# High and low fp32r parts for the experts' gate and up products, and 71 tiles instead of 72

## The reference

```python
def reference(x, cond, Wq, Wo, router_w, gate_up_w, down_w, shared_gate_w, shared_up_w, shared_down_w):
    return x + ffn(attention(x, cond, Wq, Wo))      # x: 16 x 256 x 512, float32

def attention(x, mask, Wq, Wo):                     # 8 heads of 32, over the 512 positions
    q = x.transpose(0, 2, 1) @ Wq.T                 # queries, keys and values are the same q
    logits = (scale * q_h @ q_h.T * mask_k + (1 - mask_k) * -1e30) * mask_q
    return ((softmax(logits) @ q_h) @ Wo.T).transpose(0, 2, 1)

def ffn(h):                                         # 4096 tokens of 512, 8 experts of 256, 2 a token
    shared = silu(x @ shared_gate_w) * (x @ shared_up_w) @ shared_down_w
    top_val, top_idx = top_k(x @ router_w, 2)
    probs = zeros.at[top_idx].set(sigmoid(top_val))
    gu = einsum('etd,edf->etf', probs.T[:, :, None] * x[None], gate_up_w)
    gate, up = split(gu, 2)
    return shared + einsum('eti,eid->etd', silu(gate) * up, down_w).sum(0)
```

## Time and profile before

| | us |
|---|---|
| median of the runs | 1277.66 |
| the profiled execution | 1280.32 |
| its span | 1278.2 |
| PE busy | 1192.3 (93%) |
| POOL busy | 782.2 (61%) |
| DVE busy | 696.6 (55%) |
| ACT busy | 491.7 (38%) |

### The profile page before, as it was taken

The page is one execution under the profiler, slowest core; times in us unless marked ns, Lnnn a source line. Parts: engine busy times, 40 slices in busy tenths (PEclk is TensorE's granted clock), DMA queues, the critical chain, the costliest instruction groups (busy, mean ns, idle before and its releaser), DMA issues. The chain is left out here.

```text
span 1278.2 us, 20836 instructions
## 1 busy us (share of the span) xinstructions
PE 1192.3 (93%) x5372; PEld 648.1 (51%) x5373; DVE 696.6 (55%) x1243; ACT 491.7 (38%) x922; POOL 782.2 (61%) x526
## 2 busy tenths in 40 slices
PE   4999999999999999999977999699999999999995
PEld 2444545455444555455437999544444444444442
DVE  4776676776766766667615744234444443343333
ACT  1465665665565656556543222011111111111110
POOL 1487877877877877778860277435545445444443
PEclk8799999999999999999988999899999999999998
DMA  6467667677676676685515995534454555556551
GB/s 185 137 169 210 187 171 205 175 183 205 175 195 184 171 200 190 169 215 151 151 69 199 365 359 180 170 102 139 144 162 157 174 177 173 186 184 198 190 201 50
DMA packets 116747, 230.26 MB, mean 180 GB/s; under 512 B 19230, under 2 KB 22046, under 8 KB 116704
## 3 DMA queue, kind: packets, MB, share of 16 engines
q1 hardware_dynamic: 85216, 160.35, 42.6%
q0 software_dynamic: 23936, 54.72, 14.1%
q10 hardware_dynamic: 7552, 14.68, 3.6%
HBM read 150.14 MB, written 98.39 MB: 194 GB/s over the span
## 5 line engine op out<-in xcount | busy, mean ns | idle before, releaser
L762 DVE TENSOR_REDUCE row_max<-bank 128x1 f32<-128x512 f32 x512 | 343.4, 684 | 177.4 <-PE bank L582 176.6
L695 ACT ACTIVATE probsT<-bank 128x512 f32<-128x512 f32 x512 | 300.1, 596 | 227.6 <-PE bank L594 225.5
L451 POOL TENSOR_TENSOR key_sum<-key_sum,probsT 128x1024 f32<-128x1024 f32 x128 | 299.5, 2367 | 0.4 <-ACT probsT L695 0.4
L582 PE MATMUL bank<-k_stack,q_stack 96*128 96x512 f32 x512 | 282.3, 555 | 12.8 <-DMA q_stack<-q_hi 8.1
L1506 PE MATMUL bank<-gate_up_sb,rows_T 128*128 x576 | 273.0, 597 | 1.6 <-ACT rows_T L1453 1.6
L447 POOL TENSOR_TENSOR key_sum<-probsT 128x1024 f32<-128x1024 f32 x64 | 151.3, 2377 | 129.1 <-ACT probsT L695 129.1
L594 PE MATMUL bank<-q_stack,k_stack 99*128 99x512 f32 x512 | 207.4, 406 | 1.7 <-ACT probsT L695 1.5
L1371 POOL DMA_INDIRECT out<-rows_final,slot_info x72 | 73.4, 1020 | 187.4 <-DVE rows_final L1429 185.2
L582 PEld LDWEIGHTS bank<-k_stack,q_stack 96*128 96x128 f32 x512 | 98.5, 193 | 168.4 <-DVE row_max L762 126.4
L1460 ACT ACTIVATE gated<-bank 128x256 f32<-128x256 f32 x72 | 27.6, 383 | 360.4 <-PE bank L1506 360.4
L1506 PEld LDWEIGHTS bank<-gate_up_sb,rows_T 128*128 128x128 f32 x576 | 104.5, 192 | 106.3 <-issue 106.3
(11 more groups left out here) (139 smaller groups left out, 1365.3 us busy)
## 6 DMA issues: line engine op xcount, KB each, us to landing
expert_rows_dram<-zero_rows SPq DMA_DIRECT2D x16, 1152.0 KB, 7.2
expert_rows_dram<-rows_out SPq DMA_DIRECT2D x72, 256.0 KB, 2.3
k_stack<-hi_dram SPq DMA_DIRECT2D x60, 256.0 KB, 6.6
q_stack<-hi_dram SPq DMA_DIRECT2D x60, 256.0 KB, 7.1
x_row<-in_x SPq DMA_DIRECT2D x16, 512.0 KB, 3.8
rows_ext_dram<-hid SPq DMA_DIRECT2D x16, 512.0 KB, 5.7
hidT_dram<-hidT SPq DMA_DIRECT2D x16, 512.0 KB, 3.0
tok<-hidT_dram SPq DMA_DIRECT2D x16, 512.0 KB, 5.7
```

What stands on the lines that cost most here:

```text
L451: nc.gpsimd.tensor_tensor(total, total, probs(k), ALU.add).then_inc(added, 1)
L582: nc.tensor.matmul(logit_bank[i % 2][:, :], q_stack[par][g][0:K_LOGIT, h, q * P:(q + 1) * P], k_stack[par][g][0:K_LOGIT, h, :], start=True ...
L695: nc.scalar.activation(probsT[:, j, :], key_bank[j % 2][:, :], ACT.Exp, scale=SCALE).then_inc(probs_ready, 1)
L762: nc.vector.tensor_reduce(row_max[g][:, i:i + 1], logit_bank[i % 2][:, :], AX.X, ALU.max)\
```

## The change

NT falls from 72 to 71, in all that is derived from it. The experts' gate and up weights stay in SBUF as fp32 and are split, chunk k by chunk k, while the first tiles run: ACT rounds four pieces of 128 x 1024 into `gate_up_lo[k]` (`round_pieces`), DVE replaces them by raw minus rounded (`lower_pieces`), ACT then rounds the raw weights in place (`round_in_place`). Tile n uses fp32r parts for the chunks that are split by then (one from tile 1, two from tile 3, three from 5, all four from tile 7). A split chunk is three fp32r matmuls (high x high, high x low, low x high) in place of one fp32 matmul. The rows are turned unscaled, ACT's `copy_in` makes their high part, DVE's `lower_rows` the low part. The probability is applied in silu's scale and in `combine`; `scale_rows` is gone. `turn_in(n + 1)` moves into the middle of `gate_up(n)`. DEPTH falls from 6 to 4 and AHEAD from 3 to 2. The last tile isn't stored to `expert_rows`. The text of `clear_rows` is unchanged: with NT = 71 its n is 568, r is 8, and 71 partitions are read.

```diff
-        NT = -(-(2 * TOKENS + E * (P - 1)) // (4 * P)) * 4
+        NT = (2 * TOKENS + E * (P - 1)) // P
...
-            DEPTH = 6
-            AHEAD = 3
+            DEPTH = 4
+            AHEAD = 2
+            PIECES = 4
+            EP = E // PIECES
+            FIRST_SPLIT = [2 * k + 1 for k in range(KT)]
...
+            def split_chunks(n):
+
+                return KT if not isinstance(n, int) else sum(n >= m for m in FIRST_SPLIT)
...
             @block3.vector
             def _(dve):
-                def scale_rows(n):
-                    dve.wait_ge(gathered[n % DEPTH], 16 * (n // DEPTH + 1))
-                    if n >= 2:
-                        dve.wait_ge(in_turned, n - 1)
-                    nc.vector.tensor_scalar(rows_scaled[n % 2][:, :], rows_in[n % DEPTH][:, 0, :],
-                                            slot_info[:, n, PROB:PROB + 1].bitcast(F32), None, ALU.mult).then_inc(scaled, 1)
...
+                def lower_rows(n):
+
+                    c = split_chunks(n)
+                    dve.wait_ge(in_copied, n + 1)
+                    if n >= 2:
+                        dve.wait_ge(gu_done, n - 1)
+                    nc.vector.tensor_tensor(rows_lo[n % 2][:, 0:c, :], inT_bank[n % 2][:, 0:c * P].rearrange("p (k c) -> p k c", k=c),
+                                            rows_hi[n % 2][:, 0:c, :].bitcast(F32), ALU.subtract).then_inc(in_lowered, 1)
...
+                lower_pieces(0, range(PIECES))
                 for n in range(NT + 2):
-                    if 0 <= n - 2:
+                    if 0 <= n - 2 < NT - 1:
                         add_rest(n - 2)
                     if 0 <= n - 1 < NT:
                         copy_h(n - 1)
+                    if n == NT - 1:
+                        combine(n)
                     if 0 <= n - 2:
                         add_partner(n - 2)
-                    if n < NT:
+                    if n + 1 < NT and split_chunks(n + 1):
+                        lower_rows(n + 1)
+                    if n < NT - 1:
                         combine(n)
-                    if n + 2 < NT:
-                        scale_rows(n + 2)
+                    if n < 2 * (KT - 1):
+                        lower_pieces(n // 2 + 1, range(n % 2 * PIECES // 2, (n % 2 + 1) * PIECES // 2))
 
             @block3.scalar
...
+                act.wait_ge(experts_loaded, 2 * E * 16)
+                round_pieces(0)
                 copy_in(0, 0)
-                tiles(act, step)
+                round_pieces(1)
+                for n in range(NT):
+                    if n + 1 < NT:
+                        copy_in(n + 1, n % 2 + 1)
+                    if n + 1 in FIRST_SPLIT[0:2]:
+                        round_in_place(n // 2)
+                    silu(n, n % 2)
+                    if n + 1 in FIRST_SPLIT[2:]:
+                        round_in_place(n // 2)
+                    if n in (1, 3):
+                        round_pieces(n // 2 + 2)
...
                     for k in range(KT):
-                        if k == KT // 2 and exists(n - 1):
-                            turn_h(n - 1, i - 1)
-                        w = gate_up_sb[:, bass.ds(e * KT + k, 1), :].rearrange("p o f -> p (o f)")
-                        last = nc.tensor.matmul(gu_bank[i % 2][:, :], rows_T[i % 2][:, k, :], w,
-                                                start=(k == 0), stop=(k == KT - 1))
+                        if k == KT // 2:
+                            if exists(n - 1):
+                                turn_h(n - 1, i - 1)
+                            if exists(n + 1):
+                                turn_in(n + 1, i + 1, r)
...
+                        if isinstance(n, int) and n == FIRST_SPLIT[k]:
+                            pe.wait_ge(chunk_split, PIECES * (k + 1))
+                        w_lo = gate_up_lo[k][:, bass.ds(e, 1), :].rearrange("p o f -> p (o f)")
+                        nc.tensor.matmul(dst, hi, w, start=start, stop=False)
+                        nc.tensor.matmul(dst, hi, w_lo, start=False, stop=False)
+                        last = nc.tensor.matmul(dst, lo, w, start=False, stop=stop)
                     last.then_inc(gu_done, 1)
```

More of the change, by code:

```diff
@@ L1326, in build, with tiles, piece @@
             block3 = experts.enter_context(nc.Block())
[L1328 to L1336, removed]
+            def tiles(eng, step, unroll):
+                first_round = -(-8 // unroll)
+                last_round = (NT - 2) // unroll
+                for n in range(first_round * unroll):
+                    step(n, n % unroll, n // unroll)
+                with eng.Fori(first_round, last_round) as r:
+                    for i in range(unroll):
+                        step(unroll * r + i, i, r)
+                for n in range(last_round * unroll, NT + 3):
+                    step(n, n % unroll, n // unroll)
+            def split_chunks(n):
+                return KT if not isinstance(n, int) else sum(n >= m for m in FIRST_SPLIT)
+            def piece(k, p):
+                return slice(EP * p * KT + k, (EP * (p + 1) - 1) * KT + k + 1, KT)
             def first(n, m=2):
@@ L1452, in copy_in @@
                         act.wait_ge(gu_done, n - 1)
[L1453 to L1454 removed]
+                    turned = inT_bank[i % 2][:, :].rearrange("p (k c) -> p k c", k=KT)
+                    if c < KT:
+                        last = nc.scalar.activation(rows_raw[i % 2][:, c - i % 2:, :], turned[:, c:, :], ACT.Copy)
+                    if c > 0:
+                        last = nc.scalar.activation(rows_hi[i % 2][:, 0:c, :], turned[:, 0:c, :], ACT.Copy)
@@ new lines, in copy_in, with round_pieces, round_in_place @@
+                    last.then_inc(in_copied, 1)
+                def round_pieces(k):
+                    for p in range(PIECES):
+                        nc.scalar.activation(gate_up_lo[k][:, EP * p:EP * (p + 1), :], gate_up_sb[:, piece(k, p), :], ACT.Copy)\
+                            .then_inc(piece_rounded, 1)
+                def round_in_place(k):
+                    act.wait_ge(piece_lowered, PIECES * (k + 1))
+                    if k < KT - 1:
+                        act.wait_ge(raw_used, k + 1)
+                    else:
+                        act.wait_ge(gu_done, FIRST_SPLIT[k])
+                    for p in range(PIECES):
+                        nc.scalar.activation(gate_up_hi[:, piece(k, p), :], gate_up_sb[:, piece(k, p), :], ACT.Copy).then_inc(chunk_split, 1)
@@ L1456, in silu @@
                 def silu(n, i):
                     act.wait_ge(gu_done, n + 1)
-                    if not first(n):
-                        act.wait_ge(h_done, n - 1)
-                    nc.scalar.activation(gated[i % 2][:, :], gu_bank[i % 2][:, 0:I], ACT.Silu).then_inc(silu_done, 1)
-                def step(n, i):
-                    if exists(n):
-                        silu(n, i)
-                    if exists(n + 1):
-                        copy_in(n + 1, i + 1)
-                copy_in(0, 0)
@@ L1470, in _, with step @@
             @block3.sync
             def _(sp):
-                def step(n, i):
-                    if exists(n - 2):
+                def step(n, i, r):
+                    if exists(n - 2) and not (isinstance(n, int) and n - 2 == NT - 1):
                         sp.wait_ge(out_ready, n - 1)
@@ L1477, in step @@
                             .then_inc(stored[i % 2], 16)
-                tiles(sp, step)
+                tiles(sp, step, 2)
                 for i in range(2):
-                    sp.wait_ge(stored[i], 8 * NT)
+                    sp.wait_ge(stored[i], 16 * ((NT - i) // 2))
             @block3.tensor
```

83 lines of the change are left out of this document (58 added, 25 removed).

## The result

The changed kernel takes 1906.9 us (median of 4 runs, 1906.3 to 1910.9) where the kernel before takes 1279.0 beside it: a ratio of 1.4915, 95% interval 1.4884 to 1.4946. Half as much again, slower; the forecast was 1848 us. The profiled execution took 1906.25 us with a span of 1904.5.

The account below looks back on a forecast made before the run. It took the experts to be bound by a circle of POOL, transfer and DVE, 0.26 us a tile longer than PE's work. 1280.3 + 573 + 3.5 - 6.5 = 1850.3, less 2.7: 1848 us; range 1695 to 2085.

Parts of the forecast that it names:

- One engine for a clear: Attention: each 71-partition clear runs on one DMA engine and delays what follows; +573 us, chance 0.85.
- The block of 50 us: Attention's clears: one engine moves 568 packets at 85 to 97 ns, 48 to 55 us; 50 taken.
- 36.5 us a batch: Attention: row maxima land 57 us after the clear's issue instead of 20.5; 15 batches late by 36.5, 548 us.
- End of the block, +25: Attention after the sixteenth clear: stores of the last two batches end the block near 698 us instead of 672.6.
- The signs: Profile after: clears landing near 50 us, their SP issue tens of us long, low DMA share, batch near 76 us.
- Three passes, 0: Experts' gate and up: PE falls from 5.81 to 5.3 us a tile, 36 us less work, all hidden; gain 0.
- The circle: Experts: scatter, partner gather, landing, `rows_final` and round again set the tile pace, 6.07 us, 0.26 above PE's work.
- Splitting at the start, +3.5: Experts' first tiles: rounding and lowering weight pieces delays tile 5's partner gather by 3.5 us; bounds 0 and +12.
- The end, -6.5: Experts' end with 71 tiles: the last tile's 5.0 us goes and about 1.5 of a POOL wait is spared.
- Clears that stay spread: Rival in attention: clears still land in under some 20 us, leaving 1274.6 us, no slower; chance 0.09.
- PE's pace at 1226: Rival: clears stay spread and the experts' tile period falls to 5.3 us, 49 us less, about 1226; chance 0.02.
- The new waits at 1294: Rival: clears stay spread, but `lower_rows` or later gathers stretch the experts' period by 0.3 us, +19; chance 0.04.

Follow-up runs that it names:

- Even clears: The changed kernel, still 71 tiles, with each clear writing 576 rows from 96 partitions, the last overlapping its neighbour: 1279.1 us, ratio 0.9995.
- the swap: POOL issues tile n-1's partner gather ahead of tile n-2's scatter: kernel before 1263.1 us; changed kernel with 96-partition clears 1232.0, with 72 tiles 1232.5.

## Why the prediction was right

**One engine for a clear, +573 in the sum.** Right in kind, 9% short: +627.8 us to the first gather. By its parts:

- *Does a transfer need equal shares?* I took the end in which it does, and that decided the case: 71 partitions against 72 is 636 us, and the window inside the block shows one engine busy. By the rule in the Trainium skill, "DMA: Bandwidth & Descriptors", section on why a DMA increments its semaphore by 16, which the prediction cited, 71 gives one engine, 72 twelve, 2 and 4 two and four, 8 eight. The rises of the semaphore agree in each case, and so do the DMA shares of 0.07, 0.12, 0.13 and 0.23.
- *The block of 50 us.* Right. A packet takes 84 ns inside the block in the trace (85 as read from rows 10, 48 us in all), and the clear lands 47.5 us after its issue.
- *Which transfer is late.* I named the row maxima. PE stands for a stack load first, 35.26 us, from 149.4 on; the maxima follow once it runs. The maxima's time was still right, since 187.70 + 1.8 is 56.3 us after the clear, against the 57 worked out.
- *36.5 us a batch.* This is the term that was mis-sized. Measured: 42.4 us in the batch shown, 40.7 as the mean of fifteen (611.0 / 15). The late arrival is as worked out (56.3 less 20.5 is 35.8); what failed is that the 20.6 us of work from the maxima to the next clear would be "as before". It is 27.1 us, because TensorE comes back at half its clock. I had put a slow restart into the upper bound only, and it was there after each wait looked at, the one of 4.21 us too. 15 x 4.2 is 63 us too little.
- *End of the block, +25.* +17.6 up to the first gather, 7 us too much in the sum. The 63 less these 7, and less the 0.8 us at the start, make the 55 us by which 573 falls short of 627.8.
- *The signs.* Three came out otherwise than written. The clear's own issue on SP isn't long, the next two are. The list of issues shows no landing near 50 us but none at all. And the batch is not the clear plus some 27 us but plus 31.6 (79.1 less 47.5), which is mostly the restart again.

**Three passes, 0.** Right: 1278.3 us with 72 tiles. The circle was shown by opening it. Its period was not quite untouched, though: from partner gather 9 to 66 it is 342.2 us after and 346.7 before, 4.5 us less. Of the 0.08 us a tile, 0.06 lie between the gather's issue and `rows_final` (3.15 in place of 3.21); why, no run tells.

**Splitting at the start, +3.5.** Measured 3.7 (partner gather 5 is 53.1 us behind the first gather; before, 49.4). With the circle open it costs 7.9 (55.3 against 47.4), for then nothing hides it.

**The end, -6.5.** This term had the wrong sign. The last tiles give 5.3 us up to the last partner gather, and then the end of the block takes 6.9 us back, which no row of before could show: +1.5 in all. Against it stand the 4.5 us of shorter periods and 2.2 more between partner gathers 5 and 9, which the sum didn't have, so the stage as a whole came out near the forecast (-1.5 for -3.0) partly by luck. Even clears with 71 tiles measured 1279.1 and not the 1274.6 of the first rival; 2.0 of these 4.5 us are the kernel before, 1279.7 beside it in place of 1277.66.

**The rivals.** Clears that stay spread: false as a forecast; once the clears were spread by hand, its gain of 3.1 us on the kernel before was 0.6. PE's pace at 1226: false while the circle stands; with the circle opened by the swap, 1232. The new waits at 1294: false; the period didn't grow, so `lower_rows` and the gather two tiles ahead cost nothing that shows.

## What to carry to other kernels

A size that looks like a saving (71 for 72) may be a factor in the shape of a transfer elsewhere: look through everything that is computed from it, and at the factors of the result. When a faster engine changes nothing, look for the circle of waits that sets the pace and ask which of its members needn't stand in it; here one swap in a queue gave 1.3% in the old kernel and 3.6% with the change, against nothing for the change alone. The version to keep is the three passes with the partner gather first and clears from 96 partitions: 1232 us.

## What the runs showed of the hardware that I had not expected

- Two and four DMA engines that read neighbouring SBUF partitions move 26 to 27 GB/s together, as one engine does; two that read partitions 0 and 64 move 51.
- A wait of 4.21 us costs TensorE 6.4 us more behind it (5.6 in the mean of its batches), at the granted clock 0.50 for 16.7 us in which it is busy throughout, about as much as a wait of 35 us does.
- SP doesn't stand in the transfer that blocks but in the next issues: 38.59 us in two stack loads behind a clear that it issued in 0.79 us. It is let go at 173.28, some 7 us before the clear lands at 180.65, and the loads' last data comes behind that.
- The number of engines shows in the semaphore: 2 rises for a clear from 71 partitions, 13 from 72, 16 from 96.
- The block's end on GpSimd took 7 us longer in the kernels with 71 tiles.
